# Output rows of a GRU turned by VectorE in 32x32 blocks instead of TensorE and ScalarE, sent in runs of 128 bytes; five attention group buffers instead of four

## The reference

```python
scale, shift = split(cond @ W_emb + b_emb)
xn = rms_norm(x, g_norm) * (1 + scale) + shift
q, k, v = split(xn @ W_qkv)                  # 16 heads of 32
o = softmax(rms_norm(q, g_q) @ rms_norm(k, g_k).T * 32**-0.5) @ v
x1 = x + o + o @ W_out
h = cond                                     # GRU over the 512 tokens of x1
for t in range(512):
    gi = x1[:, t] @ W_ih + b_ih
    gh = h @ W_hh + b_hh
    r, z = sigmoid(gi_r + gh_r), sigmoid(gi_z + gh_z)
    n = tanh(gi_n + r * gh_n)
    h = (1 - z) * n + z * h
    out[:, t] = x1[:, t] + h
```

## Time and profile before

| | |
|---|---|
| time, median of 3 runs | 2167.67 us (2160.76 to 2167.81) |
| profiled execution: time, span | 2156.04 us, 2154.3 us |
| granted TensorE clock | 0.999 |
| TensorE busy, share of the span | 2119.3 us, 98% |
| VectorE busy | 1299.9 us, 60% |
| ScalarE busy | 1142.4 us, 53% |

### The profile page before, as it was taken

One profiled execution on the slowest core, in us unless ns is written; L12 is line 12 of the kernel. 1 busy time (PEld: TensorE's weight loads), 2 busy tenths in 40 slices (PEclk: granted clock), 3 DMA queues, 4 the chain that ended last, 5 costly groups with the idle time before them and its releaser, 6 DMA issues.

```text
span 2154.3 us, 131481 instructions
## 1 busy us (share of the span) xinstructions
PE 2119.3 (98%) x58481; PEld 1709.9 (79%) x58481; DVE 1299.9 (60%) x4971; ACT 1142.4 (53%) x5115; POOL 188.2 (9%) x227
## 2 busy tenths in 40 slices
PE   8999999999999999999999999999999999999997
PEld 5665666656888888888888888888888888888776
DVE  4775766666466555565656665566656565666555
ACT  4775766655354544545544554454555455454544
POOL 4443333331000000000000000000000000000000
PEclk9999999999999999999999999999999999999999
DMA  6000000004200101010000001010101000010000
GB/s 223 1 21 2 1 21 2 2 1 136 95 26 23 30 15 29 17 29 20 24 23 21 27 16 34 13 32 15 29 17 30 20 24 25 19 30 18 24 4 14
DMA packets 47237, 62.10 MB, mean 29 GB/s; under 512 B 8241, under 2 KB 40525, under 8 KB 46669
## 3 DMA queue, kind: packets, MB, share of 16 engines
q1 hardware_dynamic: 45652, 50.38, 7.5%
q0 software_dynamic: 528, 3.15, 0.4%
q10 hardware_dynamic: 488, 0.15, 0.0%
HBM read 29.80 MB, written 16.78 MB: 22 GB/s over the span
## 4 chain that ended last, share of the span: by engine, by line
PE 94%; DVE 2%; ACT 1%; issue 1%; POOL 1%; DMA 0%; SPq 0%; DVEq 0%; POOLq 0%; ACTq 0%
PE ps L638 63%; PE ps L379 7%; PE ps L535 7%; PE ps L471 7%; PE ps L556 3%; PE ps L572 3%; PE ps L441 2%; PE ps L455 1%; PE ps L446 1%; PE ps L662 1%; DVE nT L1016 1%; DVE xb L1027 1%; DVE ps L1021 0%; ACT xb L817 0%; DMA x1T<-in_L_cond_W_emb 0%
## 5 line engine op out<-in xcount | busy, mean ns | idle before, releaser
L638 PE MATMUL ps<-wqkv,xb 128*4 128x128 f32 x49152 | 1483.2, 273 | 12.3 <-DVE xb L1027 8.9
L638 PEld LDWEIGHTS ps<-wqkv,xb 128*4 128x4 f32 x49152 | 1235.7, 87 | 224.5 <-DVE xb L1027 183.4
L1016 DVE STREAM_TRANSPOSE rzT<-ps 128x128 f32<-128x128 f32 x512 | 163.2, 319 | 347.1 <-PE ps L638 347.1
L822 ACT ACTIVATE r_pair<-rzT 128x8 f32<-128x8 f32 x512 | 107.7, 210 | 444.0 <-DVE rzT L1016 444.0
L1027 DVE TENSOR_TENSOR_SCAN xb<-z_trip,xb 128x24 f32<-128x24 f32 x1024 | 213.1, 208 | 188.4 <-ACT xb L817 129.8
L817 ACT ACTIVATE xb<-ps 128x16 f32<-128x16 f32 x1024 | 190.7, 186 | 163.2 <-DVE ps L1021 152.3
L781 ACT ACTIVATE probs<-ps,negmax 128x512 f32<-128x512 f32 x256 | 173.5, 690 | 105.6 <-DVE negmax L955 105.5
L471 PE MATMUL ps<-wih,x1T 128*32 128x192 f32 x3392 | 226.6, 326 | 0.2
L829 ACT ACTIVATE z_trip<-znT 128x8 f32<-128x8 f32 x512 | 109.4, 214 | 188.0 <-DVE znT L1016 187.6
L535 PE MATMUL ps<-wqkv,xnT 128*128 128x384 f32 x512 | 204.4, 487 | 1.0 <-ACT xnT L727 1.0
L798 ACT ACTIVATE ps<-seeds 128x256 f32<-128x256 f32 x512 | 194.3, 380 | 0.0
(11 more groups left out here) (86 smaller groups left out, 1415.7 us busy)
## 6 DMA issues: line engine op xcount, KB each, us to landing
gi_spill<-gi_image SPq DMA_DIRECT2D x64, 192.0 KB, 2.3
seeds<-gi_spill SPq DMA_DIRECT2D x226, 32.0 KB
seeds<-gi_spill SPq DMA_DIRECT2D x282, 16.0 KB
seeds<-blank SPq DMA_DIRECT2D x10, 384.0 KB, 3.3
out<-xb SPq DMA_DIRECT2D x60, 64.0 KB
wih<-in_L_cond_W_ih SPq DMA_DIRECT2D x1, 3072.0 KB, 14.9
xb<-in_x SPq DMA_DIRECT2D x3, 1024.0 KB, 5.4
seeds<-blank SPq DMA_DIRECT2D x1, 3072.0 KB, 20.6
```

Source lines behind the costliest of these rows:

```text
L638: last = nc.tensor.matmul(ps[QD * j:QD * j + B, bank, 0:P], hist_flat[:, first:first + 3 * B - 2:3], weights, start=False, stop=False, ski ...
L1016: return nc.vector.transpose(into[:].rearrange("p (r k b s) -> p k r s b", r=4, k=blocks, b=B, s=2), ps[:, bank, first:first + QD * blocks])
```

## The change

The output rows. For all blocks but the last, VectorE turns the block in two instructions, `turn_rows`, one at u = 3 and one at u = 5 of the next block. It turns every 32x32 square in place, so 32 tokens land on the 32 partitions of a quarter and the rows of a token stand spread over four quarters of the partitions in runs of 32 features (128 bytes). SP sends each block in 16 DMAs (batch by quarter) of 128 such runs, two in each of the loop's passes u = 7 to 14. TensorE's products and ScalarE's copies for these blocks go, and with them the waits of TensorE for `rows_ready`; the last block keeps them.

The group buffers. `oT` has five of them, used in turn, so a group's write waits only for the last reader of the buffer five groups back.

The start. SP issues the load of x[1] ahead of `wout`, `wih` and the eight bias loads, which now stand behind it in the pass b = 0; `sum_squares` of x[1] moves from u = 7 and 8 to u = 4 and 5.

The start of the recurrence. The first `open_banks` counts `banks_open` too, so `seed(0)` waits for it alone, and `seed(1)` for the second.

```diff
-        oT = sb("oT", [P, G, T])
+        oT = sb("oT", [P, G + 1, T])
...
+        group_of = lambda b, g: (b * G + g) % (G + 1)
...
+        TURN_STEPS, SEND_STEP, LAST_BLOCK = (3, 5), 7, N_BLK - 1
...
@ SyncE
             sp.wait_ge(ld_wqkv_rest, 48)
-            sp.dma_start(wout[:], nat(W_out)).then_inc(ld_wout, 16)
-            sp.dma_start(wih[:], nat(W_ih)).then_inc(ld_wih, 16)
...
                 sp.wait_ge(s["xT_ready"], (b * KT + KT))
                 sp.wait_ge(s["xr_ready"], b * TT + TT)
                 if b < B - 1:
                     sp.dma_start(xb[:], x[b + 1].rearrange("(t p) f -> p t f", p=P)).then_inc(ld_x, 16)
+                if b == 0:
+                    sp.dma_start(wout[:], nat(W_out)).then_inc(ld_wout, 16)
+                    sp.dma_start(wih[:], nat(W_ih)).then_inc(ld_wih, 16)
+                    load_biases()
...
-            def send_rows(m, b):
-                sp.wait_ge(s["rows_ready"], KT * (m + 1))
-                sp.dma_start(out[b, m * BLK:m * BLK + BLK, :], out_rows[BLK * b:BLK * b + BLK, :]).then_inc(st_out, 16)
+            def send_rows(m, b, i):
+                sp.wait_ge(s["rows_turned"], 2 * (m + 1))
+                sp.dma_start(out[b, m * BLK:m * BLK + BLK, :].rearrange("t (c i x) -> i t c x", c=KT, x=QD)[i],
+                             out_rows[QD * i:QD * i + QD, :].rearrange("t (c b x) -> t b c x", b=B, x=QD)[:, b]).then_inc(st_out, 16)
...
-                if m > 0 and 24 <= u < 24 + B:
-                    send_rows(m - 1, u - 24)
+                if m > 0 and SEND_STEP <= u < SEND_STEP + 2 * B:
+                    b, i = divmod(2 * (u - SEND_STEP), 4)
+                    send_rows(m - 1, b, i)
+                    send_rows(m - 1, b, i + 1)
...
@ TensorE
-            open_banks((0, 1, 2, 4, 5))
+            open_banks((0, 1, 2, 4, 5)).then_inc(s["banks_open"], 1)
...
-                        if b == 1 and n >= 3:
-                            pe.wait_ge(s["rows_ready"], KT * (n - 2))
...
-                if m > 0 and 13 <= u < 13 + KT:
-                    if u == 13:
-                        pe.wait_ge(s["out_added"], BLK // ADD * m)
...
-                    rows_of_block(m - 1, u - 13).then_inc(s["rows_ps"], 1)
...
@ ScalarE
-                if b < B - 1 and u in (7, 8):
+                first = 4 if b == 0 else 7
+                if b < B - 1 and u in (first, first + 1):
                     act.wait_ge(ld_x, 16 * (b + 2))
-                    sum_squares((0, 1) if u == 7 else (2, 3))
+                    sum_squares((0, 1) if u == first else (2, 3))
...
             seed(0)
+            act.wait_ge(s["banks_open"], 2)
             seed(1)
...
-                if m > 0 and u in (17, 18):
-                    if u == 17:
-                        act.wait_ge(st_out, 16 * B * (m - 1))
-                    act.wait_ge(s["rows_ps"], KT * (m - 1) + KT)
-                    copy_rows(2 * (u - 17))
-                    copy_rows(2 * (u - 17) + 1)
...
@ VectorE
-                    if b > 0:
-                        dve.wait_ge(s["ox_ready"], b * KT)
-                        dve.wait_ge(s["y_done"], b * KT)
-                    nc.vector.tensor_tensor(oT[:, g, :], ps[:, PO, :], rT_sb[:, g % 2, :], ALU.mult).then_inc(s["oT_ready"], 1)
+                    if b * G + g > G:
+                        dve.wait_ge(s["ox_ready"], b * G + g - G)
+                        dve.wait_ge(s["y_done"], KT * ((b * G + g - G - 1) // G + 1))
+                    nc.vector.tensor_tensor(oT[:, group_of(b, g), :], ps[:, PO, :], rT_sb[:, g % 2, :], ALU.mult).then_inc(s["oT_ready"], 1)
...
+            def turn_rows(m, pair):
+                dve.wait_ge(s["out_added"], BLK // ADD * (m + 1))
+                if m > 0 and pair == 0:
+                    dve.wait_ge(st_out, 16 * 4 * B * m)
+                nc.vector.transpose(out_rows[:, 2 * P * pair:2 * P * pair + 2 * P].rearrange("p (c b x) -> p c b x", c=2, x=QD),
+                                    x1T[:, 2 * pair:2 * pair + 2, :, BLK * m:BLK * m + BLK]).then_inc(s["rows_turned"], 1)
...
+                if m > 0 and u in TURN_STEPS:
+                    turn_rows(m - 1, TURN_STEPS.index(u))
```

More of the change, by code:

```diff
@@ L247, in _, with load_biases @@
             sp.wait_ge(ld_wqkv_rest, 48)
-            sp.dma_start(wout[:], nat(W_out)).then_inc(ld_wout, 16)
-            sp.dma_start(wih[:], nat(W_ih)).then_inc(ld_wih, 16)
[L250 to L255, removed]
+            def load_biases():
+                for j in range(4):
+                    quarter = slice(QD * j, QD * j + QD)
+                    for tile, source in ((b_in, b_ih), (b_hid, b_hh)):
+                        sp.dma_start(tile[quarter, :].rearrange("p (n x) -> p n x", x=QD),
+                                     source.rearrange("(n j x) -> j n x", j=4, x=QD)[j].partition_broadcast(QD)
+                                     ).then_inc(ld_bias, 16)
             for b in range(B):
@@ L315, in _ @@
                     spill(*evac_steps[step - 1])
-                if m > 0 and 24 <= u < 24 + B:
-                    send_rows(m - 1, u - 24)
-            sp.wait_ge(s["rows_ready"], KT * N_BLK)
+                if m > 0 and SEND_STEP <= u < SEND_STEP + 2 * B:
+                    b, i = divmod(2 * (u - SEND_STEP), 4)
+                    send_rows(m - 1, b, i)
+                    send_rows(m - 1, b, i + 1)
+            sp.wait_ge(s["rows_ready"], KT)
             sp.dma_start(out[:, T - BLK:T, :], out_rows).then_inc(st_out, 16)
-            sp.wait_ge(st_out, 16 * B * (N_BLK - 1) + 16)
+            sp.wait_ge(st_out, 16 * 4 * B * LAST_BLOCK + 16)
         @block.gpsimd
@@ L440, in out_projection @@
                 for k in range(KT):
-                    last = nc.tensor.matmul(ps[:, bank, :], wout[:, k, P * c:P * c + P], oT[:, k, :],
+                    last = nc.tensor.matmul(ps[:, bank, :], wout[:, k, P * c:P * c + P], oT[:, group_of(b, k), :],
                                             start=(k == 0), stop=(k == KT - 1))
@@ L446, in quarter_projection @@
                 return nc.tensor.matmul(ps[:, bank, P * c:P * c + P], wout[:, k, P * c:P * c + P],
-                                        oT[:, k, P * q:P * q + P], start=(k == 0), stop=(k == KT - 1))
+                                        oT[:, group_of(b, k), P * q:P * q + P], start=(k == 0), stop=(k == KT - 1))
             GATES_RZ, GATE_N = slice(0, 2), 2
@@ L836, in _ @@
                     seed(step + 2)
-                if m > 0 and u in (17, 18):
-                    if u == 17:
-                        act.wait_ge(st_out, 16 * B * (m - 1))
-                    act.wait_ge(s["rows_ps"], KT * (m - 1) + KT)
-                    copy_rows(2 * (u - 17))
-                    copy_rows(2 * (u - 17) + 1)
-            act.wait_ge(st_out, 16 * B * (N_BLK - 1))
+            act.wait_ge(st_out, 16 * 4 * B * LAST_BLOCK)
             for c in range(KT):
-                act.wait_ge(s["rows_ps"], KT * N_BLK)
+                act.wait_ge(s["rows_ps"], KT)
                 copy_rows(c)
@@ L896, in normalize_last @@
                 dve.wait_ge(s["r_ready"], LAST_GROUP + q + 1)
-                nc.vector.tensor_tensor(oT[:, G - 1, tokens], ps[:, PO, tokens], rT_sb[:, 1, tokens],
+                if q == 0:
+                    dve.wait_ge(s["ox_ready"], (B - 1) * G - 1)
+                    dve.wait_ge(s["y_done"], FULL_Y)
+                nc.vector.tensor_tensor(oT[:, group_of(B - 1, G - 1), tokens], ps[:, PO, tokens], rT_sb[:, 1, tokens],
                                         ALU.mult).then_inc(s["oq_ready"], 1)
```

11 lines of the change are left out of this document (3 added, 8 removed).

## The result

The changed kernel takes 2152.89 us, median of 7 runs (2149.17 to 2155.74); before, now over 7 runs, 2166.12 us (2160.76 to 2177.84). The ratio is 0.9938, with a 95% interval of 0.992 to 0.9957: faster by 0.6%. The profiled execution took 2152.64 us (span 2150.9), 3.4 us less than the one of before. That is a quarter of the difference between the medians (13.2 us), so one pair of executions is not enough here.

The account below looks back on a forecast made before the run. The prediction saw each recurrence step as a latency loop with little TensorE slack. Its terms, 2.6 + 1.2 + 0.8 + 5.0 + 4.8 - 1.5 = 12.9 us, took 2167.7 to 2154.8, rounded to 2154 us; range 2147 to 2161.

Parts of the forecast that it names:

- The group buffers: Attention slots (1, 10), (2, 10), (3, 10): the `oT` write no longer waits for its slot's y piece; gain 2.6 us.
- x[1] and its squares: Attention slots (0, 7) and (0, 8): ScalarE's squaring moves into its earlier idle time; gain 1.2 us, bounds 0.5 and 1.2.
- The first steps: Start of the recurrence: step 0 follows the last bank sooner, ScalarE's table load slightly late; gain 0.8 us.
- The products: Recurrence, u = 13 to 16 of 13 blocks: undisturbed steps shorten from 3.163 to 3.067 us; gain 5.0 us.
- The stalls that go with them: Recurrence, u = 13 to 22: TensorE's excess instruction-issue stalls go with the row products; gain 4.8 us, ends 0 and 6.6.
- rival 1: Recurrence: the stalls are not the rows' doing, so that term is 0; 2158 to 2160 us, chance 0.25.
- VectorE: Recurrence, u = 3 and 5: two 0.45 us transposes a block fit VectorE's idle gap before the rzT transpose; cost 0.
- The sends: Recurrence, SP's burst behind u = 5: may slow TensorE's instruction packets; cost 1.5 us, at most 3.
- Rival 2: Recurrence: bursts of sends starve TensorE of instructions; 2186 us, chance 0.05 of slower, 0.04 of only eating the gain.

Follow-up runs that it names:

- e1: The change without its row part (output rows by TensorE and ScalarE as before), against the kernel before: 2151.15 us, ratio 0.9972.
- e5: The change plus TensorE's 16 row products at u = 29 to 0, result unused, against the kernel before: 2155.43 us, ratio 0.9992.
- e6: The change plus twice the row products at u = 13 to 16, result unused, against the kernel before: 2166.12 us, ratio 1.0051.
- e3b: The change with its transposes but without the sends of blocks 0 to 14, against the kernel before: 2144.51 us, ratio 0.9932.
- e3: The change without transposes and sends of blocks 0 to 14, against the kernel before: 2143.20 us, ratio 0.9933.
- c1: The unaltered change measured again as control, against the kernel before: 2146.63 us, ratio 0.9957.
- e10: The change with the last block also turned by VectorE and sent in 16 DMAs from SP and ScalarE, against the kernel before: 2144.30 us, ratio 0.994.

## Why the prediction was right, step by step

- **The group buffers**, forecast 2.6 us: the three slots fell by 1.11, 1.13 and 0.33. Right. The 0.5 us that might have come back did not.
- **x[1] and its squares**, forecast 1.2: 15.04 - 13.82 = 1.22. Right. The cover was less tight than feared, since the load landed in 5.4 us, not 6.5. The last bank comes 4.10 us earlier, so the slots behind the changed ones gave 0.3 us that no term had.
- **The first steps**, forecast 0.8: the first rzT is 0.97 us closer to the last bank, and step 0 is longer by 0.14, which is what comes through of the table load's delay of 0.25 us (forecast as 0.2 or 0.3). Right. e1, these three alone, gained 6.0 us by its ratio (3.0 to 8.8), 5.1 by its profile.
- **The products**, forecast 5.0: undisturbed windows of 12.27 against 12.65, 13 times, 4.9. Right.
- **The stalls that go with them**, forecast 4.8 (all of the 3.0 in the steps with rows, half of the 3.6 behind them): 5.0, by ten-step windows with and without the products, wherever these stand. Right, and rival 1 is refuted by e5. The mechanism (TensorE runs without slack, so its instruction supply falls behind) has two supports: the waits for issue move with the products, and all of them end 1.2 to 1.6 us after an instruction packet. Against its simple form stands e6, where double the products brought 2.9 us of stalls and not 5 to 12.
- **VectorE**, forecast 0: 0.42 us in the gap, 0.41 us left. Right (e3b against e3, and the median steps u = 3 and 5).
- **The sends**, forecast 1.5 at 3 at the most: 3 by the windows, 1 to 5 by the times. The term was mis-sized, and its mechanism (slower instruction packets) is not shown: those packets took 1.09 us in the burst and 1.07 before. I priced an issue of 128 runs at 0.37 us, from a DMA of long runs; it takes 0.60 (median) and 0.79 (mean of the twelve), so the burst lasts three steps and not one and a half.
- **Rival 2** priced the packets at the mean of q1, 0.057 us, and would have filled the DMA engines. The packets of 128 bytes took 0.012 us each. The queue shows 31,680 more packets for a share of 7.9% instead of 7.5%, and a share of 0.15 in the burst. Refuted by a wide margin.
- **The Trainium skill.** The Trainium skill says that a fetch of instructions hides behind the issue ("Runtime: NRT & Kernel Launch", "Instruction fetch mechanics"). This kernel's traces differ: the change has 17.7 us of waits for issue in front of the weight loads of its steps, in 63 pieces, and each ends 1.2 to 1.6 us after an instruction packet. The loss below 512 B that the Trainium skill names ("DMA: Bandwidth & Descriptors", "Specifications") may be there for each run, no run here isolates it, but the engines had room for it at a share of 0.15.

With the measured terms the sum is 2.6 + 1.2 + 0.8 + 4.9 + 5.0 - 3 = 11.5 us. The first comparison gave 0.0062 of 2166 us, 13.4, the second (c1) 9.3; the intervals of both hold 11.5. That the forecast of 2154 came within 1.1 us of the measured 2152.89 is partly luck: the same kernel, measured twice, differs by 4 us in what it gains. The first pair of profiles gave 3.4 because the profiled execution of before, at 2156.04, was 4.7 us below the shortest of its seven timed runs, while that of the change stood at the median of its own. Why is not shown; in the later rounds before had medians of 2155.9 to 2157.7.

## What to carry over

Where a loop is bound by latency, work hung into an engine's slack costs only what sticks out of it, but work that uses up the slack costs again, in stalls that had been absorbed: here as much as its own length for the dose at hand, and less for twice the dose. Look at the length of the undisturbed iteration and at the total beyond it as two numbers. And price a DMA issue neither by its bytes nor by its number of runs, but from a DMA of the same access pattern: 128 runs of 1536 bytes took 0.34 us to issue (the spills), 512 runs of 2 KB 0.37 (the load of x[1]), 128 runs of 128 bytes, four from each partition, 0.60 (the sends). Which property of the pattern sets it was not isolated.

## What the hardware showed beyond that

- An issue of 128 runs of 128 bytes takes SP 0.79 us in the mean of a row of twelve, with a median of 0.60; 0.63 and 0.68 us where SP and ScalarE issue eight each at the same time (e10). So the two queues issue side by side: sixteen sends in 5.4 us.
- A VectorE transpose in 32x32 blocks takes 0.42 us for 256 columns from SBUF to SBUF and 0.69 for 512.
- One and the same kernel had 16 us of stalls in its recurrence in one profile and 25 in another, at a granted clock of 0.998 and 0.999, which is the 2.4 GHz level.
- In this loop TensorE's waits for instructions end 1.2 to 1.6 us after an instruction packet has ended (53 of 53 in before, 74 of 74 in the change), and the packets come every 3.8 us.
